# Graph-network kernel: shares of the last product in twos, chunk 5's sums kept in PSUM, two more pairs of chunk 6 multiplied twice

## What is computed

```python
def ggc(x, adj, W, wih, whh, bih, bhh):           # gated graph layer, used twice
    m = adj @ (x @ W)
    gi, gh = m @ wih.T + bih, x @ whh.T + bhh      # each split in r, z, n
    r, z = sigmoid(i_r + h_r), sigmoid(i_z + h_z)
    n = tanh(i_n + r * h_n)
    return (1 - z) * n + z * x
h = relu(ggc(x, ..1)); x = layernorm(x + relu(ggc(h, ..2)))
# last layer: weights from the position of each nonzero in its row of adj
rank = cumsum(adj != 0, axis=1); deg = rank[:, -1:]; k = minimum(deg, 100)
pos = rank - (deg - k)
w = (adj != 0) * where(pos > 0, 0.5 ** (k - pos), 0)
out = layernorm(x + w @ (x @ weight) + bias)
```

## Time and profile before

| | us |
|---|---|
| median of 3 runs (lowest, highest) | 375.72 (375.42, 377.91) |
| the profiled execution | 376.38 |
| its span | 374.7 |
| PE busy | 350.6 (94%) |
| DVE busy | 301.1 (80%) |
| ScalarE busy | 152.6 (41%) |
| loaded and stored | 117.38 MB, mean 313 GB/s |

### The profile page before, as it was taken

One profiled execution on the slowest core, in us unless ns is written; L12 is line 12 of the kernel. 1 busy time (PEld: TensorE's weight loads), 2 busy tenths in 40 slices (PEclk: granted clock), 3 DMA queues, 4 the chain that ended last, 5 costly groups with the idle time before them and its releaser, 6 DMA issues.

```text
span 374.7 us, 6469 instructions
## 1 busy us (share of the span) xinstructions
PE 350.6 (94%) x2424; PEld 156.1 (42%) x2424; DVE 301.1 (80%) x476; ACT 152.6 (41%) x185; POOL 25.6 (7%) x32
## 2 busy tenths in 40 slices
...
GB/s 232 405 393 389 409 380 408 372 409 366 401 409 365 393 318 407 356 356 335 348 378 329 385 352 390 350 352 343 349 360 369 374 357 242 30 0 4 2 58 58
DMA packets 36366, 117.38 MB, mean 313 GB/s; under 512 B 4208, under 2 KB 8560, under 8 KB 36336
## 3 DMA queue, kind: packets, MB, share of 16 engines
...
## 4 chain that ended last, share of the span: by engine, by line
PE 70%; DMA 16%; ACT 6%; DVE 4%; issue 2%; POOL 1%; SPq 1%; POOLq 0%; DVEq 0%; ACTq 0%
PE m_acc L435 40%; DMA stream<-in_adj_t 14%; PE out L435 12%; PE out L540 6%; PE rz_ps L513 3%; PE rz_ps L499 2%; DMA hx<-in_x_pairs 2%; PE rz_ps L492 2%; ACT codes L690 2%; PE n_ps L492 2%; PE m_acc L467 1%; ACT s_mid L690 1%; ACT stream L690 1%; DVE codes L1022 1%; POOL rstd L781 1%
## 5 line engine op out<-in xcount | busy, mean ns | idle before, releaser
L435 PE MATMUL m_acc<-stream,s_in 128*64 128x512 f32 x512 | 127.7, 611 | 7.1 <-DMA stream<-in_adj_t 6.5
L840 DVE TENSOR_SCALAR codes<-stream 128x1024 uint8<-128x1024 f32 x128 | 83.8, 686 | 13.8 <-DMA stream<-in_adj_t 13.6
L435 PE MATMUL m_acc<-stream,s_mid 128*64 128x512 f32 x280 | 67.6, 604 | 0.8 <-DMA stream<-in_adj_t 0.7
L435 PEld LDWEIGHTS m_acc<-stream,s_in 128*64 128x64 f32 x512 | 33.2, 138 | 75.1 <-issue 48.9
L435 PE MATMUL out<-stream,s_mid 128*64 128x512 f32 x232 | 58.9, 598 | 0.4 <-DMA stream<-in_adj_t 0.4
L781 POOL TENSOR_TENSOR rstd<-var,mhalf 128x4 f32<-128x4 f32 x16 | 23.7, 1484 | 345.4 <-DVE var L990 345.4
L886 DVE SCALAR_TENSOR_TENSOR codes<-codes,run 128x1024 uint32<-128x1024 uint32 (+2 forms) x36 | 39.8, 1107 | 1.2
L881 DVE TENSOR_TENSOR run<-run,codes 128x2048 uint16<-128x2048 uint16 (+2 forms) x35 | 38.4, 1098 | 1.2
L690 ACT ACTIVATE wexp<-codes,code_bias 128x2048 uint16<-128x2048 uint8 x18 | 35.7, 1990 | 1.9 <-PE out L540 1.9
L622 ACT ACTIVATE m_high<-m_acc 64x512 f32<-64x512 f32 x14 | 8.3, 594 | 57.4 <-PE m_acc L435 47.2
L690 ACT ACTIVATE codes<-codes,code_bias 128x2048 uint16<-128x2048 uint8 x16 | 31.6, 1987 | 0.0
...
## 6 DMA issues: line engine op xcount, KB each, us to landing
stream<-in_adj_t SPq DMA_DIRECT2D x212, 512.0 KB, 6.5
...
```

The lines of the kernel that those rows point to most:

```text
L435: last = nc.tensor.matmul(to[D * u:D * (u + 1), :], state[:, t * D:(t + 1) * D], stream[:, n % SLOTS, u * CW:(u + 1) * CW], start=start[u] ...
L840: nc.vector.tensor_scalar(edges(p // 2, b, 2 * (p % 2), 2), stream[:, n % SLOTS, :], 0.0, None, ALU.not_equal).then_inc(mask_made, 1)
```

## The change

Four things, all in the order of work and in the places of sums; what is computed stays the same.

1. `TRI[6]` becomes 5: in pass 1, chunk 6 multiplies two more pairs twice (10 instead of 8), and pass 2 loads two pairs less (82 instead of 84; 210 loads in all instead of 212).
2. `KEPT` becomes chunks 2 to 4. Chunk 5's second sums stay in the bank `out3`, and stretch s=2 adds to them there. One `keep_copy`, one `keep_add` and one identity product are gone. To free the banks, `count` uses one bank instead of two, and `M2_BANK` and waits are set anew.
3. `TURN` holds 12 pairs: chunk 7's last two stand at places 8 and 9 of the list instead of 10 and 11, with chunk 6's last three behind them. `ALONG_PAIRS` is 11, 12, 12, 12, 12, 11 instead of 12, 12, 12, 12, 12, 13.
4. `SHARE_AT` is (0, 0, 3, 3): two shares right behind `gates`, two right behind `node`. DVE's tiles are spread anew: a third one is begun early in chunk 6, stretch 1 has tiles 4 to 8 instead of 4 to 7, stretch 5 has four instead of five.

```diff
-TRI = (0, 0, 2, 3, 4, 4, 4, 5)
-KEPT = range(2, 6)
+TRI = (0, 0, 2, 3, 4, 4, 5, 5)
+KEPT = range(2, 5)
+M2_BANK = {2: 2, 3: 1, 4: 2, 5: 3, 6: 1, 7: 2}
+M2_AFTER = {4: 2, 6: 3, 7: 4}
...
-TURN = [(0, 10), (0, 11), (0, 12), (0, 13), (1, 8), (1, 9), (1, 10), (1, 11), (1, 12),
-        (0, 14), (0, 15)]
+TURN = [(0, 10), (0, 11), (0, 12), (0, 13), (1, 10), (1, 11), (1, 12), (0, 14), (0, 15),
+        (1, 13), (1, 14), (1, 15)]
...
-CHAIN_EARLY = {6: {12: 1, 14: 1}, 7: {9: 1, 12: 1}}
+CHAIN_EARLY = {6: {12: 1, 13: 1, 15: 1}, 7: {9: 1, 12: 1}}
...
-ALONG_PAIRS = {1: 12, 2: 12, 3: 12, 4: 12, 5: 12, 6: 13}
+ALONG_PAIRS = {1: 11, 2: 12, 3: 12, 4: 12, 5: 12, 6: 11}
...
-SHARE_AT = {2: (0, 1, 4, 6), 3: (0, 1, 4, 6), 4: (0, 1, 4, 6), 5: (0, 1, 4, 6), 6: (0, 1, 4, 6)}
+SHARE_AT = {t: (0, 0, 3, 3) for t in range(2, 7)}
...
-CHAIN = [chain_tiles(*x) for x in ((0, 4), (4, 8), (8, 12), (12, 16), (16, 20), (20, 25), (25, 30),
+CHAIN = [chain_tiles(*x) for x in ((0, 4), (4, 9), (9, 13), (13, 17), (17, 21), (21, 25), (25, 30),
...
-            return m2_bank(2 * NCH - 1 - g) if g in (NCH, NCH + 1) else m_acc[g % 2]
+            return m2_bank(2 * NCH - 1 - g) if NCH <= g <= NCH + 2 else m_acc[g % 2]
...
-                first = s >= 2 and q == 2 * TRI[ch]
+                first = s >= 3 and q == 2 * TRI[ch]
...
-                if b >= 2:
-                    pe.wait_ge(start_made, b - 1)
-                nc.tensor.matmul(count_ps[b % 2][:, :], tri[:, :], s_bf[:, :],
+                if b >= 1:
+                    pe.wait_ge(start_made, b)
+                nc.tensor.matmul(count_ps[:, :], tri[:, :], s_bf[:, :],
```

More of the change, by code:

```diff
@@ L54 @@
          [0, 8, 1, 9, 2, 10, 3, 11, 6, 12, 7, 13, 4, 14, 5, 15],
-         BY_TURNS, BY_TURNS, BY_TURNS,
-         [0, 10, 1, 11, 2, 12, 3, 13, 4, 14, 5, 6, 7, 15, 8, 9]]
+         BY_TURNS, BY_TURNS] + [[0, 10, 1, 11, 2, 12, 3, 13, 4, 14, 5, 6, 7, 15, 8, 9]] * 2
 QUADS = [(slice(0, 2), slice(2, 4), slice(4, 6), slice(6, 8))] * 2 + \
     [(slice(0, 4, 2), slice(4, 6), slice(1, 4, 2), slice(6, 8))] + \
-    [(slice(0, 2), slice(4, 6), slice(2, 4), slice(6, 8))] * 4 + \
-    [(slice(0, 2), slice(5, 7), slice(2, 4), slice(4, 8, 3))]
-NEED = [(8, 12, 16)] * 2 + [(8, 15, 16)] * 5 + [(8, 13, 16)]
-TURN = [(0, 10), (0, 11), (0, 12), (0, 13), (1, 8), (1, 9), (1, 10), (1, 11), (1, 12),
-        (0, 14), (0, 15)]
-LOADS = [(b, q) for b in range(NCH) for q in PAIRS[b]] + [(NCH + s, q) for s, q in TURN] + [(NCH + 1, q) for q in (13, 14, 15)] + \
+    [(slice(0, 2), slice(4, 6), slice(2, 4), slice(6, 8))] * 3 + \
+    [(slice(0, 2), slice(5, 7), slice(2, 4), slice(4, 8, 3))] * 2
+NEED = [(8, 12, 16)] * 2 + [(8, 15, 16)] * 4 + [(8, 13, 16)] * 2
+TURN = [(0, 10), (0, 11), (0, 12), (0, 13), (1, 10), (1, 11), (1, 12), (0, 14), (0, 15),
+        (1, 13), (1, 14), (1, 15)]
+LOADS = [(b, q) for b in range(NCH) for q in PAIRS[b]] + [(NCH + s, q) for s, q in TURN] + \
         [(NCH + s, q) for s in range(2, NCH) for q in range(2 * TRI[NCH - 1 - s], NP)]
@@ L448, in product1 @@
                     if first:
[L449 removed]
+                        if b == 5:
                             pe.wait_ge(to_sup_made, 4)
[L451 to L452 removed]
+                        if b in M2_AFTER:
+                            pe.wait_ge(m2_kept, KEPT.index(M2_AFTER[b]) + 1)
                     last = pair(n, q, s_mid, m2_bank(b), [first] * 2, q == twice[-1] and b in KEPT)
@@ L458, in product2 @@
                 n = LOAD_AT[g, q]
-                first = s >= 2 and q == 2 * TRI[ch]
+                first = s >= 3 and q == 2 * TRI[ch]
                 pe.wait_ge(s_mid_made, q // 2 + 1)
                 if first:
-                    pe.wait_ge(m_ready, s + 5 if s < 4 else s + 7)
+                    pe.wait_ge(m_ready, {3: NCH, 4: NCH - 1}.get(s, s + 7))
                     if ch in KEPT:
```

24 lines of the change are left out of this document (11 added, 13 removed).

## The result

The changed kernel took 378.73 us in the median of 20 runs (376.44 to 380.59), the kernel before 376.06 in 20 runs beside them (374.3 to 378.11). The ratio is 1.0059, with a 95% interval of 1.0041 to 1.0078: slower by 1.5 to 2.9 us, where 0.8 us less was forecast. The profiled execution has a span of 377.2 us against 374.7.

A forecast was written before the change was run, and what follows sets the result against it. PE was taken to bound most stages, with DMA second in pass 2 and DVE holding stretch 6. Terms +1.72 - 1.3 - 0.7 - 0.5 = -0.8 us on 375.72 gave 374.9 us, range 372.3 to 378.6.

The forecast's parts named there:

- Chunk 6: Pass 1, chunk 6: two more pairs multiplied twice at 0.86 us each, nothing hides them, +1.72 us; DVE's early tile hidden.
- `TURN` and stretch 1: From `TURN` through stretch 1: stall and slow matmuls go, loads take back most; 29.35 instead of 30.65 us, -1.3.
- stall at `gates(8)`: Before stretch 1: PE's 1.46 us wait for `combine(8)` should go, with three chunk 6 pairs standing ahead of `gates(8)`.
- 1.63 us of slow clock: Behind the stall: `gates(8)` and three pairs run at a lower clock, costing 1.17 + 0.46 us, which should go.
- 0.9 to 1.0 more: Stretch 1, DVE's work: one tile more against about 1.5 us less on the narrow one, 0.9 to 1.0 us more.
- Stretches 2 to 5: Pass 2, stretches 2 to 5: PE needs about 3.4 us less, late loads give back 2.7, so -0.7 us.
- PE alone: Stretches 2 to 5 by PE's own need, without waits for loads: 69.9 us, about 3.4 less than before.
- 2.7 of 3.4 us: Stretches 2 to 5: part of PE's saving given back, by late-load waits of half a microsecond to 0.8 per stretch.
- rival (c): Runs of seven or nine pairs in stretches 2 to 5 meet late loads, 2.4 us waiting each: 382.2 us, chance 0.09.
- Stretch 6: Stretch 6: DVE's five tiles take 17.86 us, so only 0.51 of PE's 2.37 us counts, -0.5; `node(14)` waits over 2.
- Rival (b): DMA already limits pass 2; only chunk 6 and stretch 6 count: +1.2, 376.9 us; chance 0.22 with a stall-stays rival.

The follow-up runs named there:

- half_after: Changed kernel with each load of pass 2 bringing only the first half of a pair: 374.39 us, ratio 0.9942 to the kernel before.
- half_after_act: `half_after` with one of ScalarE's four expansions behind the split moved ahead of it in stretches 3 to 5: 371.69 us, ratio 0.9889.
- tile_sooner: Changed kernel with one whole DVE tile moved from stretch 6 to stretch 5: 376.5 us, ratio 1.0009 to the kernel before.
- first_even: Changed kernel with the fifth DVE tile of stretch 1 moved to stretch 4: 377.43 us, ratio 1.0042 to the kernel before.
- tiles_evened: Changed kernel with DVE's tiles dealt 4, 4, 4, 5, 5, 4 to stretches 1 to 6: 375.41 us, ratio 0.9968 to the kernel before.
- before_twos: Kernel before with only the shares moved to (0, 0, 3, 3): 376.64 us, ratio 1.0008.

## Why the prediction was wrong, point by point

**Chunk 6, right.** +1.71 us against +1.72. DVE's early tile is hidden as said.

**`TURN` and stretch 1, about right as a stage, and wrong in its parts: -0.48 in the pair of executions, not -1.3.** The stall at `gates(8)` went, as said. By `gates` the stage is held by loads: 24.9 us in `half_after` and `half_after_act`, 30.17 in the change. Eight executions share these loads, and they take 28.54 to 30.63, 29.5 in the mean, where 29.35 was forecast; the kernel before and its two variants took 30.25 to 30.65. So the 0.8 that is missing in one pair of executions is within their scatter. Two parts of the price were wrong. The 1.63 us of slow clock came from a single execution; three others with the same stall don't have them, and the two of these with whole loads take only 0.3 and 0.4 us less. And the step "it gets 1.23 x 2 for one tile more and loses about 1.5 on the narrow one, so 0.9 to 1.0 more" added up DVE's work without its place: behind `stat` it is 1.9 us more, with 0.63 us of slack to meet it, so `t_n` of stretch 2 is late.

**Stretches 2 to 5, the step that failed: +0.62 us, not -0.7.** PE's saving is real: 73.34 us came down to 69.6 of PE alone, where 69.9 was forecast; with half loads in both kernels stretches 3 to 5 take 2.2 to 2.4 us less, where 3 x 0.65 + 0.15 = 2.1 was forecast. What failed is the price of late loads against it. The prediction let them give back 2.7 of 3.4 us, "half a microsecond to 0.8" per stretch; they cost 4.35 us in stretches 3 to 5 (1.29, 2.56 and 0.50, each against `half_after_act`), against a saving of 3.7. The prediction knew the mechanism and gave waits of 2.4 to rival (c) as a rare case; the two longest were 1.32 and 1.18 us (264.67 and 284.05), with shorter ones beside them. It is not a single bad execution: from `gates(7)` to `gates(13)`, the two terms together, the kernels with the change's loads and shares took 104.13 us (the change), 105.01 (`tile_sooner`), 102.98 (`first_even`) and 103.74 (`tiles_evened`), where 102.0 was forecast and before took 103.99. `before_twos` alone did what this term says (-0.95 in the trace). Stretches 3 to 5 take 54.31 us in it against 55.98 in the change, with the same shares. Not the late `t_n` of stretch 2, since `node(9)` does not wait in the change, but loads that are later make this difference; why they are later, the runs don't show. The loop of `h_c`, `x1s`, split and expansions is one more bound that the sum lacked: 17.8 us per stretch from `t_n` to `t_n`, 71.2 for four, where "PE alone" had 69.9.

**Stretch 6, right.** DVE's five tiles hold it at 17.78 us (17.86 forecast), and `node(14)` waits 2.40 (over 2 forecast). What I did not ask: whether this bound is the change's doing. It is not, it was there before, but only in the changed kernel does it hide PE's gain, and one tile moved gives 1.9 us.

**Behind and ahead, open.** The profiled execution was 1.10 us late at `gates(5)`, where the two kernels do the same but for the PSUM banks and the waits on them (`count` has one bank instead of two). Over all sixteen traces `gates(5)` begins at 149.16 to 149.77 us in four with two banks and at 149.27 to 150.64 in twelve with one. The ranges overlap, and the means differ by 0.6 us. PE's waits up to there are put down to loads, to `s_in` and, for 1.3 us in the change, to nothing that the profile shows ("issue"), and none to ScalarE, which frees the bank of `count`. No run undid the single bank alone, so it is open whether this is chance. It is a third of the distance between forecast and trace.

**Rivals.** Rival (b), 376.9, was nearest among them for the wrong reason: loads are late, but at over 400 GB/s in a full ring and not because 355 to 360 is a limit. Rival (c) named the mechanism, at twice its size: it had 2.4 us of waiting per stretch, and 4.35 us over four stretches are 1.1, past the 0.85 from which it said that PE's whole gain is lost. The upper end of the range, 378.6, is 0.1 us under the median. That distance means little, since the ratio of 1.0059 on the 375.72 from which the sum started is 377.9; what failed is the direction, 2.2 us more where 0.8 less was forecast. The range ended in the lower part of (c), and the sum held nothing for the loop through ScalarE.
